# Pre-LN attention and FFN on eight cores: h1 evacuated head by head, epsilon as the bias of Sqrt

## The reference

```python
x = x + attn(layernorm(x), ln_g, ln_b, Wq, bq, Wk, bk, Wv, bv)
x = x + ffn(layernorm(x), w_gate, w_up, w_down)

def attn(x, ...):
    xn = layernorm(x) * ln_g + ln_b            # eps = 1e-5
    q, k, v = xn @ Wq.T + bq, xn @ Wk.T + bk, xn @ Wv.T + bv
    q = softmax(q per head, axis=-1)           # over the 64 features of a head
    k = softmax(k per head, axis=tokens)
    attn = einsum('bnhd,bnhl->bhdl', k, v)     # 16 heads, 64 x 64 each
    return x + einsum('bnhd,bhdl->bnhl', q, attn)

def ffn(x, ...):                               # weights are int / 127, HID = 3072
    return (silu(x @ wg.T) * (x @ wu.T)) @ wd.T
```

## Time and profile before

| | us |
|---|---|
| median of 2 runs | 4338.06 |
| the two runs | 4321.39 and 4354.73 |
| profiled execution (the first of them) | 4321.39 |
| its span on the slowest core (core 2) | 4319.7 |
| spans of the other cores | 4281.0 to 4314.0 |
| phase 1 + 2, first sequence | 133 to 973 |
| phase 3, first sequence | 973 to 1203 |
| phase 1 + 2, second sequence | 1203 to 1990 |
| phase 3, second sequence | 1990 to 2288 |
| FFN | 2288 to the end |

### The profile page before, as it was taken

The page is one execution under the profiler, slowest core; times in us unless marked ns, Lnnn a source line. Parts: engine busy times, 40 slices in busy tenths (PEclk is TensorE's granted clock), DMA queues, the critical chain, the costliest instruction groups (busy, mean ns, idle before and its releaser), DMA issues.

```text
span 4319.7 us, 59616 instructions; the slowest of 8 cores (4281.0 to 4319.7 us)
## 1 busy us (share of the span) xinstructions
PE 3632.1 (84%) x22512; PEld 2444.7 (57%) x22800; DVE 1212.4 (28%) x2694; ACT 637.0 (15%) x1092; POOL 180.2 (4%) x316
## 2 busy tenths in 40 slices
PE   6698897646559879863567999999999999999998
PEld 4343333346524334343555777777777777777776
DVE  4312212145531231232452222222222222222222
ACT  3212212112221221210220000000000000000000
POOL 0000000100100001000010000000000000000000
PEclk9899878875579989986558999999999999999999
DMA  4111111474432342359544000000000000000000
GB/s 128 54 55 70 66 47 52 93 180 138 140 108 67 82 98 64 82 150 176 146 141 93 30 30 30 14 17 30 30 30 30 30 21 10 30 30 30 30 11 11
DMA packets 229558, 289.17 MB, mean 67 GB/s; under 512 B 83989, under 2 KB 182421, under 8 KB 226458
## 3 DMA queue, kind: packets, MB, share of 16 engines
q1 hardware_dynamic: 144666, 136.42, 11.6%
q0 software_dynamic: 34432, 136.33, 10.8%
q10 hardware_dynamic: 50176, 12.59, 1.9%
HBM read 167.86 MB, written 136.31 MB: 70 GB/s over the span
## 4 chain that ended last, share of the span: by engine, by line
PE 77%; DVE 9%; DMA 4%; ACT 3%; issue 3%; ACTq 2%; another core or an unknown queue 1%; DVEq 0%; POOL 0%; SPq 0%; POOLq 0%
PE pb L1121 31%; PE pb L631 16%; PE pb L1090 15%; PE pb L569 9%; ACTq L94 2%; DMA s_hnT_lo<-hnT_lo_st 2%; PE pb L789 2%; PE pb L842 1%; DVE n_t L534 1%; DVE hnT_lo_st L860 1%; DVE xnT_lo L542 1%; DMA kTe<-s_kT 1%; ACT xnT_hi L539 1%; ACT hnT_hi_st L855 1%
## 5 line engine op out<-in xcount | busy, mean ns | idle before, releaser
L1121 PE MATMUL pb<-hnT_hi_b,wgT 128*128 128x256 bf16 x3072 | 838.1, 273 | 10.0 <-DMA s_hnT_lo<-hnT_lo_st 10.0
L1121 PE MATMUL pb<-hnT_lo_b,wgT 128*128 128x256 bf16 x3072 | 838.0, 273 | 0.0
L1121 PE MATMUL pb<-hnT_hi_b,wuT 128*128 128x256 bf16 x3072 | 838.0, 273 | 0.0
L1121 PE MATMUL pb<-hnT_lo_b,wuT 128*128 128x256 bf16 x3072 | 837.9, 273 | 0.0
L1134 DVE SCALAR_TENSOR_TENSOR g_t<-pb,g_t 128x256 f32<-128x256 f32 x384 | 163.0, 424 | 1444.9 <-ACT g_t L1130 1423.8
L1090 PE MATMUL pb<-wdT_t,hmT_lo 128*128 128x512 bf16 x1536 | 457.7, 380 | 0.0
L1090 PE MATMUL pb<-wdT_t,hmT_hi 128*128 128x512 bf16 x1344 | 416.0, 379 | 17.5 <-DVE hmT_lo L1143 7.3
L1130 ACT ACTIVATE g_t<-pb 128x256 f32<-128x256 f32 x384 | 147.5, 384 | 1858.8 <-PE pb L1121 1858.7
L1121 PEld LDWEIGHTS pb<-hnT_hi_b,wgT 128*128 128x128 bf16 x3072 | 300.8, 98 | 84.6 <-issue 10.7
L1121 PEld LDWEIGHTS pb<-hnT_lo_b,wgT 128*128 128x128 bf16 x3072 | 300.8, 98 | 74.4 <-issue 0.3
L569 PE MATMUL pb<-wvT_hi,xnT_hi 128*128 128x512 bf16 x480 | 181.7, 460 | 186.5 <-DVE v_stg L599 178.8
(11 more groups left out here) (147 smaller groups left out, 3819.7 us busy)
## 6 DMA issues: line engine op xcount, KB each, us to landing
x_r<-x SPq DMA_DIRECT2D x32, 512.0 KB, 4.1
s_r<-r_r POOLq DMA_DIRECT2D x32, 512.0 KB, 4.9
s_v<-v_stg POOLq DMA_DIRECT2D x32, 512.0 KB, 3.6
s_qT<-qT_stg POOLq DMA_DIRECT2D x64, 256.0 KB, 2.7
s_kT<-kT_stg POOLq DMA_DIRECT2D x64, 256.0 KB, 2.7
kTe<-s_kT SPq DMA_DIRECT2D x16, 1024.0 KB, 6.4
v_p<-s_v SPq DMA_DIRECT2D x16, 1024.0 KB, 6.8
qT_c<-s_qT SPq DMA_DIRECT2D x32, 512.0 KB, 7.1
```

The source lines that it names most:

```text
L1121: hc=hc, bsl=bsl, st=st, sp=sp: e.matmul(pb[bnk][:, 0:256], wtt[:, d, hc * 128:(hc + 1) * 128], xt.ap()[:, bsl, d, :], start=st, stop=sp),
```

## The change

There are two edits. In `ln_stats` the VectorE instruction that adds epsilon goes, and Sqrt gets epsilon as its bias, a column `eps_t` that one memset fills in the prologue. In phase 3 the four DVE instructions that make h1 become 16, one per head: SCALAR_TENSOR_TENSOR multiplies 64 columns of PSUM by the head's column of `rq_all`, a scalar per partition, and adds the 64 columns of `r_c`. A bank is now free when its eight instructions are done, and the marker lists of the banks and of the h1 store are longer. The first of the 16 waits for `r_c`, where before only the adds did.

```diff
--- before.py
+++ after.py
@@ -205,6 +205,7 @@
     ones_bf = A("ones_bf", [1, 128], BF16, offset=2560)
     bq_col = A("bq_col", [128, 8], F32, offset=2816)
     ones2 = A("ones2", [128, 2], F32, offset=2880)
+    eps_t = A("eps_t", [128, 1], F32, offset=2944)
     brow_v_hi = A("brow_v_hi", [1, D], BF16, offset=2816 + 4 * KB)
     brow_v_lo = A("brow_v_lo", [1, D], BF16, offset=2816 + 6 * KB)
     attn_all = A("attn_all", [128, 8, 128], F32, offset=2816 + 8 * KB)
@@ -404,6 +405,7 @@
             out=rlo[0:1, :], in0=brow[w][0:1, :], in1=rhi[0:1, :]),
             waits=m_brow[w] + [mh_])
         m_btile[w] = [mh_, ml_]
+    m_eps = P.op("vector", lambda e: e.memset(eps_t[:], EPS))
     mz2 = P.op("vector", lambda e: e.memset(ones2[:], 0.0))
     mo2a = P.op("vector", lambda e: e.memset(ones2[0:64, 0:1], 1.0), waits=[mz2])
     m_ones2 = P.op("vector", lambda e: e.memset(ones2[64:128, 1:2], 1.0),
@@ -446,12 +448,9 @@
             out=stat.ap()[:, 38:44], in_=src_ap[:, 512:1024]), waits=dep_markers)
         mag = P.op("vector", lambda e, ms=mean_slot: e.bn_aggr(
             out=stat[:, ms:ms + 2], in_=bnv), waits=[mb1, mb2])
-        mvp = P.op("vector", lambda e, ms=mean_slot: e.tensor_scalar_add(
-            out=stat[:, ms + 2:ms + 3], in0=stat[:, ms + 1:ms + 2],
-            scalar1=EPS), waits=[mag])
         msr = P.op("scalar", lambda e, ms=mean_slot: e.activation(
-            out=stat[:, ms + 3:ms + 4], in_=stat[:, ms + 2:ms + 3],
-            func=AF.Sqrt), waits=[mvp])
+            out=stat[:, ms + 3:ms + 4], in_=stat[:, ms + 1:ms + 2],
+            func=AF.Sqrt, bias=eps_t[:]), waits=[mag, m_eps])
         mrc = P.op("vector", lambda e, ms=mean_slot, rs=rstd_slot: e.reciprocal(
             out=stat[:, rs:rs + 1], in_=stat[:, ms + 3:ms + 4]), waits=[msr])
         return mrc
@@ -917,31 +916,24 @@
                     yms.append(mmy)
             flush_hn()
             hevs = []
-            bfree = []
-            for half in range(2):
-                bnk = b0 + half
-                hs = slice(half * 512, (half + 1) * 512)
-                rq_bc = bass.AP(rq_all.ap().tensor, c * 16 + half * 8,
-                                [[CPS * 16, 128], [1, 8], [0, 64]])
-                mmul = P.op("vector",
-                            lambda e, bnk=bnk, hs=hs, sl=sl, rq_bc=rq_bc:
-                            e.tensor_tensor(
-                                out=h1_st.ap()[:, sl, hs].rearrange(
-                                    "p (h x) -> p h x", x=64),
-                                in0=pb[bnk].ap()[:, :].rearrange(
-                                    "p (h x) -> p h x", x=64),
-                                in1=rq_bc, op=OP.mult),
-                            waits=[yms[half], mrq] + h1_res[sl].free)
-                bfree.append(mmul)
-                madd = P.op("vector",
-                            lambda e, hs=hs, sl=sl: e.tensor_add(
-                                out=h1_st[:, sl, hs],
-                                in0=h1_st[:, sl, hs],
-                                in1=r_c[:, sl, hs]),
-                            waits=[mmul, mr])
-                hevs.append(madd)
-            bank[b0].free = [bfree[0]]
-            bank[b0 + 1].free = [bfree[1]]
+            for p_ in range(8):
+                bnk = b0 + p_ // 4
+                for hh in range(2):
+                    head = 2 * p_ + hh
+                    cs = slice(p_ * 128 + hh * 64, p_ * 128 + (hh + 1) * 64)
+                    ps = slice((p_ % 4) * 128 + hh * 64,
+                               (p_ % 4) * 128 + (hh + 1) * 64)
+                    mh = P.op("vector",
+                              lambda e, bnk=bnk, cs=cs, ps=ps, head=head, c=c,
+                              sl=sl: e.scalar_tensor_tensor(
+                                  out=h1_st[:, sl, cs], in0=pb[bnk].ap()[:, ps],
+                                  scalar=rq_all[:, c, head:head + 1],
+                                  in1=r_c[:, sl, cs], op0=OP.mult, op1=OP.add),
+                              waits=[yms[p_ // 4], mr, mrq]
+                              + h1_res[sl].free)
+                    hevs.append(mh)
+            bank[b0].free = hevs[:8]
+            bank[b0 + 1].free = hevs[8:]
             rc_res[sl].free = [hevs[-1]]
             qc_res[sl].free = yms[:] + [sqm]
             mh1 = P.dma("gpsimd", s_h1[tok0:tok0 + 128, :], h1_st[:, sl, :],
```

## The result

The changed kernel is slower. The rest took 4432.78, 4445.30 and 4449.37 us, before 4320.99 to 4354.73 (7 executions, median 4345.67): a ratio of the changed kernel to before of 1.0234, 95% interval 1.0185 to 1.0282. So it is slower, and this comparison alone leaves open whether by over or under 2%. On the median of before the ratio is 102 us, where the sum gave 81. The same kernel, run again on two chips, came to 1.0187 both times (1.0166 to 1.0207, and 1.0167 to 1.0207), which is 81 us on 4338. That leaves two questions: whether the 81 us are the ones that were worked out, and where the first comparison had 20 more from.

What follows compares the result with a forecast made beforehand. No engine is full in phase 3, so a chain of latencies sets the pace; +88.0 us over 31 chunks, -6.3 for stores and -0.7 in phase 1 give +81.0, on the median 4338.06 to 4419 us; widened range 4386 to 4446.

Steps and rivals of the forecast that it cites:

- the sum: Whole kernel: +88.0 us in phase 3, less 6.3 of late stores and 0.7 in phase 1, +81.0 us.
- That h_st and the epsilon add are links of the chain in every chunk: Phase 3: both rewritten VectorE pieces lie on the chain PE waits for; PE's transposes start after 4.76 us of idling.
- Rival C: Phase 3: the block has slack, so only the Sqrt edit shows, 4332 us; chance 0.04.
- The instruction: Phase 3 h_st: each 64-column instruction takes 283 ns, 223 without pointer plus 60 for the pointer scalar.
- Rivals A: Phase 3 h_st: pointer costs VectorE 91 ns as on ScalarE, 314 to 315 ns each, 4436 us; chance 0.21.
- B: Phase 3 h_st: pointer fetched beside the streams, 223 ns each, +53 us, 4391 us; chance 0.14.
- The gap: Between h_st instructions: 0.10 us of semaphore wait, period 0.391, 16 take 6.26 us, +3.01 us per chunk.
- The epsilon edit: ln_stats: 0.26 us saved before Sqrt, 0.09 added by its bias pointer, net -0.17 us per chunk; -0.7 us in phase 1.
- 31 chunks, not 32: Phase 3: second sequence's first chunk waits for ACT's queue, 3 us vanish in 50; 31 x (3.01 - 0.17) = +88.0 us.
- The stores: Phase 3, even chunks: transposes' 6.8 us of waiting for late hnT stores is absorbed but for 0.5, -6.3 us.
- The waits that come with the change cost nothing: Phase 3: 14 more waits on PE, about 1 us a chunk, are hidden in 4.76 us of idling; without slack, 32 us.
- set the sum on the median: Whole kernel: the 33 us between two executions of before is scatter shared by both kernels, so 4338.06 becomes 4419 us.

Runs made afterwards that it cites:

- the two staging tiles alone: Kernel before with hnT_hi and hnT_lo staged in two tiles each, h_st left in its place, against before: ratio 0.9982, 8 us less.
- third set: The changed kernel with no further edit, run a third time, on the next chip, against before: ratio 1.0187 (1.0167 to 1.0207).
- the shorter lists: Changed kernel with each bank freed by its last instruction and the h1 store waiting for the last of 16: ratio 1.0191 to before, no difference from the changed kernel.

## Why the prediction was right in its sum and wrong in its time

Point by point, by its own steps:

- **That h_st and the epsilon add are links of the chain in every chunk:** right, and shown from both sides, by the changed kernel (+80.6 us of phase 3) and by taking the block out of the chain by its place alone (97 us less with two staging tiles). Rival C falls.
- **The instruction:** 283 ns forecast, 283 measured. The pointer costs 58 ns (283 against 225), where L449 and L490 gave 60. Rivals A and B both fall: neither 294 ns nor 223.
- **The gap:** 0.391 us apart forecast, 0.388 measured (6.20 over 16), so the block grew by 2.95 us and not by 3.01. The stages agree: the 16 instructions alone and the two staging tiles alone, neither of which waits for stores, differ by 44.4 us in 15 chunks, 2.96 each.
- **The epsilon edit:** 0.17 a chunk forecast. The chain shows the 0.40 us as 0.14, and Sqrt 0.09 longer, but between two kernels that differ in it alone phase 3 differs by 0.14 a chunk, or 0.15 with h_st moved. Taken alone it gave 6 us by the ratio and 2.5 by the stages. The 0.7 us in phase 1 are shown by no run.
- **31 chunks, not 32:** right as far as can be seen. The first chunk of the second sequence takes 67 to 70 us on core 2 with either kernel. In the changed one its BN_AGGR starts at 2033.75 and its Sqrt at 2087.78, behind ACT's queue, so a block 3 us longer still has 50 us of room. Over the cores this chunk scatters by more than that (59 to 72 us before, 65 to 76 in the third set).
- **The stores:** right in kind and a little low. Their wait at the transposes is gone in the changed kernel, and two staging tiles alone give before 8 us, against the 6.8 read as excess on core 2.
- **The waits that come with the change cost nothing:** right, by the shorter lists.
- **The sum:** +81.0 us, of it +81.7 in phase 3, against +80.6 in the stages and 81 by the ratio of 1.0187 on two chips. Its terms were off by 1 to 2 us each over the 31 chunks, in both directions, so that it is right to within 1 us is in part luck.

The step that failed is the one that set the sum on the median, a scatter that was sized too small and taken as equal in both kernels: "the whole 33 us between them is scatter that the changed kernel has as well". It took two executions of before for the whole width of the scatter, when the profile in front of me had a stretch of 23 us in it (cores 2 and 3 started phase 3 at 973.3 and 971.0, the others at 945 to 952) that I had read past, and gave the range no term for one more. In its place the first comparison showed 102 us. By the spans of its cores that is the 81 and about one stretch more on the changed kernel's slowest cores than on those of before. Its middle time is 4445.30 us, 26 above the forecast of 4419: 8 because the median of before came to 4345.67 with seven executions, and 19 from the stretch. The longest, 4449.37, is above the 4446 where the range ended, and 1.0234 is over the bound of 2%, though its interval holds the bound. The price of the change itself, 1.9%, lies within the 2%. The range should have reached up by the 23 us of a stretch more, to some 4470, and a chance near one half for slower by over 2% would have been a better reading of 81 against a bound of 87.

What stays open is what sets such a stretch off, and whether a kernel with longer phases of low PE load gets more of them. Two later comparisons, on two chips, show no sign of it; the first had 102 us on three executions, and nothing here tells apart whether that was its chip or luck.

## What to carry to other kernels

A chain of short dependent instructions is priced by start-to-start distance: here an instruction of 64 columns costs 0.39 us by its fixed part, its pointer scalar and the wait for the one before, and only 0.07 of that are columns. Fewer bytes moved by a fused operation did not pay here, where they came in four times as many instructions. Before rewriting a block on the chain, look where it stands in its engine's queue: moving the four unchanged instructions in front of work that waits for another engine gained 97 us with a second pair of staging tiles, eight times what fusing and moving together did with the same tiles and the epsilon edit (12). With the single pair nearly half of that was given back to the stores, which were late next.

## What the runs showed of the hardware

- A pointer scalar costs a VectorE instruction 58 ns (283 against 225 ns at 64 columns), a bias pointer an ACT instruction 91 (294 against 203).
- A granted clock of 0.81 is held in stretches of some 150 us (on core 2 of before from about 500 to 650 us), by the two cores of a pair (0 and 1, 2 and 3) and not always by the die. Each costs some 23 us, and in a kernel timed by its slowest core it is as large as a good edit.
- The changed kernel's phase 3 repeated within 1.3 us over all cores of its three profiled executions (262.2 to 263.5 us), while the whole times that were compared went from 4377 to 4449. Before's, in which transposes wait for stores, differs by 5 us from core to core (217.7 to 222.7), and with two staging tiles by 0.1 (216.2 or 216.3). For an edit in one stage, the stage's length is the sharper measure where nothing in it waits for late stores.
